# A Mamba, attention and mixture-of-experts layer in one kernel: scan and attention reordered, eight exponentials in sixteen summed on VectorE, row scatters moved, and eight buffers for the last loads

## The chip, the cores and the metric

The kernel runs as one program on 1 core of a Trainium2 chip. The metric is the device time of one execution, in microseconds (us). The program has one queue of instructions for each engine: TensorE (PE, matmuls and transposes), VectorE (DVE), ScalarE (ACT), GpSimd (POOL), and SyncE (SP), which issues most DMAs. Every queue runs in the order in which it was written and waits only on semaphores; no scheduler moves anything.

## The reference, cut to what matters

The input `x` is 32 sequences of 128 tokens of 128 numbers (4096 tokens). Three blocks follow one another, each with a residual and a layernorm.

```python
# block 1: selective state-space model, 256 channels, 16 states
xs, res = split(x @ W_in)                      # 256 + 256 columns
u = silu(conv4(xs) + conv_b)                   # causal, 4 taps, per channel
dt, Bm, Cm = split(u @ W_x)                    # 64, 16, 16
delta = softplus(dt @ W_dt + b_dt)
h[t] = exp(delta[t] * A) * h[t-1] + delta[t] * Bm[t] * u[t]     # per channel and state
y = (sum_n h * Cm + u * D) * silu(res)
x = layernorm(x + y @ W_out)
# block 2: causal attention to ctx, 16 heads of 8, rotary positions
s = rope(x @ Wq.T) . rope(ctx @ Wk.T) / sqrt(8) + masks
x = layernorm(x + softmax(s) @ (ctx @ Wv.T) @ Wo.T + bo)
# block 3: 8 experts, 2 for each token, F = 512
wte = phi_routing(x @ gate_w.T)
x = layernorm(x + sum_e wte[:, e] * ((silu(x @ w1[e].T) * (x @ w3[e].T)) @ w2[e].T))
```

## The kernel before

**Groups.** The first two blocks run over G = 8 groups of S = 4 sequences, T = 512 tokens. For group `m` the code calls `w` the group before, `e` the next and `c` the one after next, since stages of several groups overlap: while group m is scanned, the convolution of c, the step sizes of e and the routing of w are done in between.

**Scan.** The 256 channels times 16 states of 512 tokens are NU = 16 units `k`. For each, ACT makes `decays` (`decay`, L673, four exponentials of 128x256), PE makes the inputs in a pair of PSUM banks (`entries`, L1436, 16 matmuls), DVE runs the recurrence (`states`, L967), and POOL multiplies by C (`times_c`, L496). After every fourth unit PE sums over the states (`y_add`, L1458). The sets alternate: units 1, 3, 5, ... take `pair_b`, the others `pair_a`, unit 0 `y_ps`. So `entries(7)` may start when scan 5 has ended, and scan 7 may start when `entries(7)` has ended. Eight places in SBUF hold the states; scan 8 also needs that `y_add(m, 0)` has emptied the first four. PE's list puts into each step k, behind `entries(k+1)`, parts of other groups: transposes of x (`x_t`), `conv`, `res`, `b_columns`, `values`, the logits of w.

**Attention.** For each sequence t of four: `scores` puts 16 heads into four banks (pair_b and y_ps, two halves k), `maxima` (DVE, L1025) takes row maxima, `exps` (ACT, L714) takes 16 exponentials of 128x128 into `prob`, each with `accum_out`, which gives the row's sum in `den`. `head_t` (PE, L1549) transposes `prob` by four heads, `pT_out` (half on ACT, L724, half on DVE, L1040) copies them out, `heads_v` (L1570) multiplies with the values. `inverses` (DVE, L1030) and `inverses_t` prepare 1/den, `normed` applies it. PE's `scores(g, t+1, k)` overwrites the banks that the exponentials of t read, so it waits for them. The queries of sequences 2 and 3 take a path of their own: `first_norm(g, 1)` (DVE, L1009), `x1_t` (PE, L1512), `x1_in` (ACT, L702), `queries` (PE, L1518), `rope_q` (DVE, L1015), `add_q` (POOL, L501); `scores(g, 2, 0)` waits for them.

**Routing.** When the experts of group w are known, `scatter` (POOL, L528) sends each token's row to the rows of its two experts in DRAM, eight indirect DMAs for a group, issued two groups later.

**Experts.** 72 tiles of 128 rows run in a software pipeline (`up`, `down`, L1742 to L1754). At the end the two result rows of each token come back in eight groups (`results_in`, SP, L407) to four buffers `yk`; group g+4 waits until group g is summed. ACT and POOL multiply by the gates (`weighted`, L896, L585), PE sums (`sums`, L1782), DVE takes statistics (L1324, L1328), ACT the root (`ln_scale3`), and DVE writes the norm (`last_norm`, L1335), which SP stores (L411).

## Time and profile before

| what | value |
|---|---|
| device time, median of 3 runs | 1009.97 us (1008.43 to 1010.68) |
| the profiled execution: its own time | 999.74 us |
| its span | 997.8 us |
| PE busy | 872.5 us (87%) |
| PE weight loads busy | 580.5 us (58%) |
| DVE busy | 742.2 us (74%) |
| ACT busy | 719.8 us (72%) |
| POOL busy | 581.1 us (58%) |
| mean granted clock of TensorE | 0.975 |

The span goes from the first instruction to the last; the profiled execution's own time is 1.9 us longer, and the median of the timed runs lies 10.2 us above it. Busy times of engines overlap. A row of the timeline begins with the start and the duration in us; the duration of a row with x4 is that of the four together, and neighbours on one engine can overlap at their ends because they are pipelined. What stands in brackets is the engine's idle time before the row, and who ended it.

### The profile page before, as it was taken

How to read it: one execution, taken by the hardware profiler on the slowest of the kernel's cores; microseconds unless marked ns; L12 is line 12 of the kernel's file. 1: busy time of each engine (PE TensorE's matmuls, PEld its weight loads, DVE VectorE, ACT ScalarE, POOL GpSimd, SP SyncE). 2: the span in 40 equal slices, each digit the busy share in tenths (PEclk: the TensorE clock that was granted, in tenths of full speed). 3: DMA queues.
4: the chain of work that ended last, by engine and by line, in shares of the span. 5: the costliest groups of instructions: out<-in, count | busy, mean ns of one | idle time of the engine just before them, and what ended most of it. 6: DMA issues, size and time to landing. Idle time of an engine off the chain costs nothing.

```text
span 997.8 us, 29713 instructions
## 1 busy us (share of the span) xinstructions
PE 872.5 (87%) x10285; PEld 580.5 (58%) x10286; DVE 742.2 (74%) x1503; ACT 719.8 (72%) x2213; POOL 581.1 (58%) x394
## 2 busy tenths in 40 slices
PE   5578988989899798889989888988898999999996
PEld 2234554454455345445544544554588999999972
DVE  2589788878878977887897797788764666666657
ACT  3597997898799689879959985965924555555556
POOL 2588359629846973984797398397152333333331
PEclk8799999999999999999999998999999999999999
DMA  3435101500610240061033006004041111111135
GB/s 106 107 66 142 41 4 48 123 16 11 151 42 14 71 112 18 9 156 37 14 86 86 19 8 154 8 13 175 7 136 52 48 48 48 48 48 46 47 118 169
DMA packets 68476, 66.12 MB, mean 66 GB/s; under 512 B 9040, under 2 KB 62480, under 8 KB 67984
## 3 DMA queue, kind: packets, MB, share of 16 engines
q1 hardware_dynamic: 63440, 55.58, 21.5%
q0 software_dynamic: 4352, 8.99, 2.7%
q8 instruction: 69, 1.13, 0.5%
q14 instruction: 39, 0.32, 0.1%
q10 hardware_dynamic: 576, 0.10, 0.1%
HBM read 48.51 MB, written 16.13 MB: 65 GB/s over the span
## 4 chain that ended last, share of the span: by engine, by line
PE 44%; ACT 21%; DVE 18%; issue 12%; POOL 3%; DMA 2%; SPq 0%; DVEq 0%; POOLq 0%; ACTq 0%
ACT prob L714 8%; PE pair_b L1746 7%; PE pair_a L1742 7%; DVE prob L967 6%; ACT decays L673 5%; DVE hst L967 4%; PE pair_b L1538 3%; PE bank L1754 3%; PE y_ps L1754 3%; PE bank L1549 3%; DVE u L933 2%; PE pair_a L1570 2%; PE pair_a L1478 2%; PE y_ps L1538 1%; PE pair_a L1436 1%
## 5 line engine op out<-in xcount | busy, mean ns | idle before, releaser
L673 ACT ACTIVATE decays<-w,a_neg 128x256 f32<-128x256 f32 x512 | 218.7, 509 | 47.1 <-DVE prob L967 30.1
L496 POOL TENSOR_TENSOR hst<-hst,c_rep 128x1024 f32<-128x1024 f32 x64 | 151.3, 2372 | 12.6 <-DVE hst L967 12.0
L576 POOL DMA_INDIRECT y<-aoT,dest x72 | 77.3, 1074 | 135.1 <-DVE aoT L1289 131.5
L496 POOL TENSOR_TENSOR prob<-prob,c_rep 128x1024 f32<-128x1024 f32 x56 | 132.1, 2368 | 9.4 <-DVE prob L967 8.9
L528 POOL DMA_INDIRECT xg<-x_all,pos x64 | 64.9, 1014 | 88.4 <-DVE pos L1117 77.1
L714 ACT ACTIVATE prob<-pair_b,nmax 128x128 f32<-128x128 f32 x256 | 90.2, 399 | 2.1 <-DVE nmax L1025 2.1
L967 DVE TENSOR_TENSOR_SCAN prob<-decays,pair_b 128x1024 f32<-128x1024 f32 x32 | 72.8, 2276 | 24.0 <-issue 18.6
L714 ACT ACTIVATE prob<-y_ps,nmax 128x128 f32<-128x128 f32 x256 | 90.6, 413 | 0.0
L1436 PE MATMUL pair_a<-w,du_tok 64*32 64x256 f32 x1792 | 63.4, 392 | 29.8 <-DVE prob L967 15.1
L1436 PE MATMUL pair_b<-w,du_tok 64*32 64x256 f32 x2048 | 71.6, 389 | 19.5 <-DVE prob L967 12.1
L488 POOL TENSOR_TENSOR w<-diag,b_tok 128x1024 f32<-128x1024 f32 x32 | 61.9, 1959 | 37.5 <-ACT b_tok L654 23.5
L1742 PE MATMUL pair_a<-qk,u 128*128 128x128 f32 x592 | 78.2, 275 | 0.0
L1746 PE MATMUL pair_b<-qk,u 128*128 128x128 f32 x592 | 78.2, 275 | 0.0
L860 ACT ACTIVATE zabs<-pair_a 128x512 f32<-128x512 f32 x74 | 44.2, 598 | 44.7 <-PE pair_a L1742 44.7
L1549 PE MATMUL bank<-ident,prob 128*128 128x128 f32 x512 | 70.7, 279 | 5.2 <-ACT pT L724 5.2
L1549 PEld LDWEIGHTS bank<-ident,prob 128*128 128x128 f32 x512 | 55.1, 140 | 31.4 <-issue 18.4
L967 DVE TENSOR_TENSOR_SCAN hst<-decays,pair_b 128x1024 f32<-128x1024 f32 x32 | 72.6, 2269 | 0.6 <-issue 0.3
L967 DVE TENSOR_TENSOR_SCAN prob<-decays,pair_a 128x1024 f32<-128x1024 f32 x32 | 72.7, 2272 | 0.2 <-PE pair_a L1436 0.2
L1746 PEld LDWEIGHTS pair_b<-qk,u 128*128 128x128 f32 x592 | 72.0, 192 | 0.0
L1742 PEld LDWEIGHTS pair_a<-qk,u 128*128 128x128 f32 x592 | 71.9, 192 | 0.0
L1436 PEld LDWEIGHTS pair_b<-w,du_tok 64*32 64x32 f32 x2048 | 31.9, 107 | 60.1 <-DVE prob L967 27.0
L714 ACT ACTIVATION_READ_ACCUMULATOR prob<-y_ps,nmax 128x1 f32 x256 | 65.1, 254 | 0.0
(291 smaller groups left out, 2194.6 us busy)
## 6 DMA issues: line engine op xcount, KB each, us to landing
w<-d_dram SPq DMA_DIRECT2D x64, 256.0 KB, 6.5
c_rep<-c_dram SPq DMA_DIRECT2D x64, 128.0 KB, 3.8
qk<-xg SPq DMA_DIRECT2D x79, 65.0 KB
d_dram<-zpos SPq DMA_DIRECT2D x8, 512.0 KB, 3.2
xn<-in_x SPq DMA_DIRECT2D x8, 256.0 KB, 2.9
cn<-in_ctx SPq DMA_DIRECT2D x8, 256.0 KB, 3.1
mask_b<-in_mask SPq DMA_DIRECT2D x8, 256.0 KB, 3.3
w<-in_w1T SPq DMA_DIRECT2D x1, 2048.0 KB, 7.8
```

The lines of the kernel that those rows point to most:

```text
L488: last = g_.tensor_tensor(b_diag[:, t], diag64[:, :].unsqueeze(1).broadcast_to((P, NST, HK)), b_tok[:, t, :].unsqueeze(2).broadcast_to((P, ...
L496: g_.tensor_tensor(by_state(ring(k)), by_state(ring(k)), c_rep[:, :, toks[r]].rearrange("p q (i t) -> p i q t", i=2), ALU.mult).then_inc(s ...
L528: pool.indirect_dma_start(xg[:, :], bass.IndirectOffsetOnAxis(ap=pos[:, t, k:k + 1], axis=0), x2_all[:, w * S + t, :], None).then_inc(s["s ...
L576: pool.indirect_dma_start(y2[:, :], bass.IndirectOffsetOnAxis(ap=dest[:, b:b + 1], axis=0), ys[:, b % 4, :], None).then_inc(s[f"y_out{b % ...
L673: last = A(by_state(decays[:, k % 3, :])[:, :, q, :], delta_rep[:, b, toks[r]].rearrange("p (i t) -> p i t", i=2), ACT.Exp, scale=a_neg[:, ...
L714: last = A(prob[:, t % 2, c, j, :], bank[2 + c][:, j * L:(j + 1) * L], ACT.Exp, bias=nmax[:, t % 2, h:h + 1], accum_out=den[:, t % 2, h:h ...
L967: v_.tensor_tensor_scan(ring(k), decays[:, k % 3, :], pair(k)[:, :, :].rearrange("p i c -> p (i c)"), 0.0, ALU.mult, ALU.add).then_inc(s[" ...
L1436: last = MM(pair(k)[32 * j:32 * j + 32, i, :].rearrange("p (q y t) -> p q y t", q=NQ, y=2)[:, :, y, :], du_tok[half, r, y, 32 * b:32 * b + ...
L1549: last = TR(bank[6 + c % 2][:, j * L:(j + 1) * L], prob[:, t % 2, c, j, :], ident[:, :])
L1742: last = MM(bank[b][:, c * P:(c + 1) * P], w13[:, b, 0, c * P:(c + 1) * P], xsT[:, b, :], start=True, stop=True)
L1746: last = MM(bank[2 + b][:, c * P:(c + 1) * P], w13[:, b, 1, c * P:(c + 1) * P], xsT[:, b, :], start=True, stop=True)
L1754: last = MM(bank[5 + b][:, 0:P], gg[:, b, c * P:(c + 1) * P], w2[:, bass.ds(e, 1), c, :].rearrange("p a d -> p (a d)"), start=(c == 0), st ...
```

## The change

No arithmetic is dropped. Five things change.

1. **Scan.** On PE, `y_add(m, 0)` moves from step 5 to step 6, so that `entries(7)` stands ahead of it; `conv(c, 0)` goes from step 5 to 7, `conv(c, 1)` from 8 to 9, `b_columns` from 6 to 7, `res` from 11 and 13 to 12 and 13. ACT's `x_in`, `conv_out` and DVE's `taps_in` move with them.
2. **Scatters.** The four of a group that stood between POOL's first scan products move into the attention, so that all eight stand there.
3. **The way from scan to attention.** On PE, `y_add(g, 3)` goes ahead of `du_t(e, 1)` and `scores(g, 0, 1)` ahead of `residual(g, 1)`. On ACT, the silu of u and its table load go ahead of `x1_in(g, 0)`, `exps(g, 0, 0)` ahead of `duT_out(e, 1)`, `ln_scale1(g, 1)` behind `exps(g, 0, 1)`, and `x1_in(g, 1)` behind `exps(g, 1, 0)`. On DVE and PE, the first sequence's work is reordered, and the queries of sequences 2 and 3 come later in it.
4. **Sums.** For t = 1, 2, 3 the first eight exponentials leave out `accum_out`; a new DVE instruction, `sums_of_exps`, reduces their 128x1024 to 128x8, and `inverses` waits for it as well.
5. **End.** `yk` has eight buffers (four in the place of `w1`), and SP issues the eight loads ahead of all stores, without waiting.

```diff
-        yk = [x.rearrange("p k (s d) -> p (k s) d", s=S) for x in (c_rep[:, 0:2, :], u[:, 0], u[:, 1], sres[:, 0])]
+
+        yk = [x.rearrange("p k (s d) -> p (k s) d", s=S)
+              for x in (c_rep[:, 0:2, :], u[:, 0], u[:, 1], sres[:, 0], w1[:, 0:2], w1[:, 2:4], w1[:, 4:6], w1[:, 6:8])]
...
-            for b in range(4):
-                results_in(b, b)
             for g in range(G):
-                if g + 4 < G:
-                    at(sp, "acc_ps", g + 1)
-                    results_in(g + 4, g % 4)
+                results_in(g)
+            for g in range(G):
                 store(g)
             for b in range(2):
...
                 for k in range(NU - 1):
-                    if m >= 2 and k < S:
-                        scatter(m - 2, (k,))
                     times_c(m, k)
...
                 if m >= 2:
-                    scatter(m - 2, (S,))
+                    scatter(m - 2, (0,))
                 if e is not None:
                     diagonals(e, 1)
                 if m >= 2:
-                    scatter(m - 2, (S + 1,))
+                    scatter(m - 2, (1, 2, 3, 4))
                 add_q(m, 1)
                 if m >= 2:
-                    scatter(m - 2, (S + 2,))
+                    scatter(m - 2, (5,))
                 add_bo(m)
                 if m >= 2:
-                    scatter(m - 2, (S + 3,))
+                    scatter(m - 2, (6,))
                 if e is not None:
                     add_k(e)
+                if m >= 2:
+                    scatter(m - 2, (7,))
+                if e is not None:
                     masked(e)
                     mask_bias(e)
...
-            def silus(c):
+            def silus_u(c):
                 nc.scalar.preload_act_table_set("silu_and_others")
                 for h in range(2):
                     u_silu(c, h)
+
+            def silus_res(c):
                 at(act, "res_sb", 2 * (c - 2) + 2)
                 A(sres[:, c % 3], sres[:, c % 3], ACT.Silu).then_inc(s["sres_sb"], 1)
                 nc.scalar.preload_act_table_set("natural_log_exp_and_others")
...
+                    mine = {} if t and not k else {"accum_out": den[:, t % 2, h:h + 1]}
+                    last = A(prob[:, t % 2, c, j, :], bank[2 + c][:, j * L:(j + 1) * L], ACT.Exp, bias=nmax[:, t % 2, h:h + 1], **mine)
...
                 if c is not None:
                     res_out(c, 1)
+                    silus_u(c)
                 x1_in(g, 0)
                 for j in range(4):
                     own_k(g, j)
                 if e is not None:
                     duT_out(e, 0, 6)
                 if c is not None:
-                    silus(c)
+                    silus_res(c)
+                exps(g, 0, 0)
                 if e is not None:
                     duT_out(e, 1, 6)
-                exps(g, 0, 0)
+                exps(g, 0, 1)
                 ln_scale1(g, 1)
-                exps(g, 0, 1)
-                x1_in(g, 1)
...
+            def sums_of_exps(g, t):
+                at(dve, "p_sb", 16 * g + 4 * t + 2)
+                at(dve, "rden_sb", S * g + t - 1)
+                v_.tensor_reduce(out=den[:, t % 2, 0:H // 2], in_=prob[:, t % 2, 0:2].rearrange("p c j m -> p (c j) m"), axis=AX.X,
+                                 op=ALU.add).then_inc(s["den_sb"], 1)
+
             def inverses(g, t):
                 at(dve, "p_sb", 16 * g + 4 * t + 4)
+                if t:
+                    at(dve, "den_sb", (S - 1) * g + t)
...
-                first_norm(g, 1)
-                if w is not None:
-                    which(w)
                 for t in range(S):
                     if t == S - 1 and w is not None:
                         ranked(w)
                         normed(g, t - 1)
                     if t + 1 < S:
                         maxima(g, t + 1, 0)
-                    if t == 0 and e is not None:
-                        rope_k(e, 0, 0)
+                    if t == 0:
+                        first_norm(g, 1)
+                        pT_out(g, t, 1)
+                        if w is not None:
+                            which(w)
+                        if e is not None:
+                            rope_k(e, 0, 0)
                     inverses(g, t)
                     if t + 1 < S:
                         widen(g, t)
                     if t and not (t == S - 1 and w is not None):
                         normed(g, t - 1)
-                    pT_out(g, t, 1)
-                    if t == 0:
-                        rope_q(g, 1)
+                    if t:
+                        pT_out(g, t, 1)
                     if t == 1 and w is not None:
                         cast(w)
                         mark(w)
-                    if t == 0 and e is not None:
-                        rope_k(e, 1, 0)
                     if t + 1 < S:
                         maxima(g, t + 1, 1)
                     elif e is not None:
                         states(e, 0)
+                    if t == 0:
+                        rope_q(g, 1)
                     pT_out(g, t, 3)
+                    if t == 0 and e is not None:
+                        rope_k(e, 1, 0)
+                    if t + 1 < S:
+                        sums_of_exps(g, t + 1)
...
-                    if k == 5:
+                    if k == 6:
                         y_add(m, 0)
                     if k == 8:
                         values(g)
...
                         if k == 3:
                             step(e, 0, 4)
                             step(e, 1, 5)
-                        if k == 6:
+                        if k == 7:
                             b_columns(e, 7)
                         if k == 14:
                             du_t(e, 0, 6)
                     if c is not None:
-                        if k == 5:
+                        if k == 7:
                             conv(c, 0, 6)
-                        if k == 8:
+                        if k == 9:
                             conv(c, 1, 6)
...
                 scores(g, 0, 0)
+                y_add(g, 3)
                 if e is not None:
                     du_t(e, 1, 6)
-                y_add(g, 3)
+                scores(g, 0, 1)
                 residual(g, 1)
-                scores(g, 0, 1)
                 first_out(g, 1)
                 if e is not None:
                     c_t(e, 0)
                 for t in range(S):
                     if t + 1 < S:
                         scores(g, t + 1, 0)
-                    if t == 0:
-                        if e is not None:
-                            keys(e, 0, 0)
-                        x1_t(g, 1)
                     if t:
                         inverses_t(g, t - 1)
                         heads_v(g, t - 1)
...
                     head_t(g, t, 0)
                     head_t(g, t, 1)
                     if t == 0:
-                        queries(g, 1)
                         if e is not None:
-                            keys(e, 1, 0)
+                            keys(e, 0, 0)
+                        x1_t(g, 1)
                     if t + 1 < S:
                         scores(g, t + 1, 1)
                     head_t(g, t, 2)
+                    if t == 0:
+                        if e is not None:
+                            keys(e, 1, 0)
+                        queries(g, 1)
                     if t == S - 1 and e is not None:
                         entries(e, 0)
```

The next two pieces are PE in the scan, steps 4 to 7 of a middle group (L1436, now L1454: `entries`; L1593, now L1611: logits; L1445, now L1463: `y_begin`; L1458, now L1476: `y_add`, of whose eight rows two stand here). Before:

```order
L1436 MATMUL pair_a<-w,du_tok 32x4x64 x16
L1593 MATMUL bank<-gate_wT,x2T 128x8 x4
L1445 MATMUL y_ps<-u,d_diag 128x256 x2
L1458 MATMUL y_ps<-hst,sum 32x256 x2
L1458 MATMUL y_ps<-prob,sum 32x256 x2
...
L1365 MATMUL bank<-xT,w_in 128x512
L1436 MATMUL pair_b<-w,du_tok 32x4x64 x16
L1398 MATMUL bank<-ident,dtl 128x32 x4
```

Now:

```order
L1454 MATMUL pair_a<-w,du_tok 32x4x64 x16
L1611 MATMUL bank<-gate_wT,x2T 128x8 x4
L1463 MATMUL y_ps<-u,d_diag 128x256 x2
L1454 MATMUL pair_b<-w,du_tok 32x4x64 x16
L1476 MATMUL y_ps<-hst,sum 32x256 x2
L1476 MATMUL y_ps<-prob,sum 32x256 x2
...
L1454 MATMUL pair_a<-w,du_tok 32x4x64 x16
L1416 MATMUL bank<-ident,dtl 128x32 x4
L1383 MATMUL bank<-xT,w_in 128x512
L1454 MATMUL pair_b<-w,du_tok 32x4x64 x16
```

The `entries` of unit 7, into `pair_b`, stood behind `y_add` and `conv` (L1365, now L1383); now it stands ahead of both, and `b_columns` and `conv` stand behind the entries of unit 8.

The next two pieces are DVE in the attention of a middle group, first sequence (L1025, now L1030: `maxima`; L1009, now L1014: `first_norm(g, 1)`; L1015, now L1020: `rope_q(g, 1)`; L1040, now L1053: `pT_out`). Before:

```order
L1009 TENSOR_SCALAR x<-pair_a,mv,rstd 128x128 x2
L1084 MAX_INDEX i<-m_all,lg_all 128x8 x4
L1025 TENSOR_REDUCE nmax<-pair_b 128x4 x2
L983 TENSOR_TENSOR rotk<-pair_a,rope 128x512
L1030 RECIPROCAL rden<-den 128x16
L1034 TENSOR_TENSOR rden_wide<-rden,one_col 128x128
L1040 COPY pT<-bank 128x512
L1015 TENSOR_TENSOR rotq<-pair_a,rope 128x256 x2
L983 TENSOR_TENSOR rotk<-pair_a,rope 128x512
L1025 TENSOR_REDUCE nmax<-y_ps 128x4 x2
L1040 COPY hst<-bank 128x512
L1025 TENSOR_REDUCE nmax<-pair_b 128x4 x2
```

Now:

```order
L1030 TENSOR_REDUCE nmax<-pair_b 128x4 x2
L1014 TENSOR_SCALAR x<-pair_a,mv,rstd 128x128 x2
L1053 COPY pT<-bank 128x512
L1097 MAX_INDEX i<-m_all,lg_all 128x8 x4
L988 TENSOR_TENSOR rotk<-pair_a,rope 128x512
L1043 RECIPROCAL rden<-den 128x16
L1047 TENSOR_TENSOR rden_wide<-rden,one_col 128x128
L1030 TENSOR_REDUCE nmax<-y_ps 128x4 x2
L1020 TENSOR_TENSOR rotq<-pair_a,rope 128x256 x2
L1053 COPY hst<-bank 128x512
L988 TENSOR_TENSOR rotk<-pair_a,rope 128x512
L1036 TENSOR_REDUCE den<-prob 128x8
```

`first_norm` stood ahead of the maxima of the next sequence and stands behind them; `rope_q` stands behind the second maxima; and a reduction of `prob` (L1036, `sums_of_exps`) ends the piece.

The last two pieces are POOL behind the scan products (L488, now L487: `diagonals`; L528, now L527: `scatter`; L501, now L500: `add_q(g, 1)`). Before:

```order
L488 TENSOR_TENSOR w<-diag,b_tok 128x1024 x2
L528 DMA xg<-x_all,pos 33920x130
L488 TENSOR_TENSOR w<-diag,b_tok 128x1024 x2
L528 DMA xg<-x_all,pos 33920x130
L501 TENSOR_TENSOR qk<-rotq 128x256
```

Now:

```order
L487 TENSOR_TENSOR w<-diag,b_tok 128x1024 x2
L527 DMA xg<-x_all,pos 33920x130
L487 TENSOR_TENSOR w<-diag,b_tok 128x1024 x2
L527 DMA xg<-x_all,pos 33920x130 x4
L500 TENSOR_TENSOR qk<-rotq 128x256
L527 DMA xg<-x_all,pos 33920x130
```

Five scatters instead of two stand ahead of `add_q(g, 1)`.

## Rows read from the trace of the kernel before

**Rows 1.** The page's chain that ended last, shares of the span by engine.

```profile
PE 44%; ACT 21%; DVE 18%; issue 12%; POOL 3%; DMA 2%; SPq 0%; DVEq 0%; POOLq 0%; ACTq 0%
```

**Rows 2.** Busy us (count) of PE, PEld, DVE, ACT, POOL by stretch; clock, DMA, GB/s.

```profile
303.40:326.10 22.70, 21.71 (x343) 12.29 (x342) 19.32 (x25) 21.04 (x50) 18.27 (x11) 1.00 0.05 15
326.10:354.60 28.50, 21.64 (x363) 10.94 (x362) 28.05 (x26) 18.56 (x43) 25.91 (x15) 1.00 0.44 103
354.60:365.50 10.90, 9.81 (x75) 5.26 (x74) 7.64 (x27) 10.83 (x41) 9.55 (x6) 1.00 0.50 135
365.50:389.40 23.90, 22.11 (x251) 13.20 (x250) 16.47 (x39) 22.50 (x110) 8.46 (x7) 1.00 0.07 19
...
760.00:964.40 204.40, 203.33 (x1823) 203.17 (x1822) 130.62 (x443) 110.57 (x219) 77.30 (x72) 1.00 0.17 47
```

**Rows 3.** Timeline of DVE, scans: start, us, and idle time before in brackets.

```profile
326.09 2.29 DVE L967 TENSOR_TENSOR_SCAN prob<-decays,pair_b 128x1024 f32<-128x1024 f32 x1 [2.86 <-issue]
...
584.09 2.29 DVE L967 TENSOR_TENSOR_SCAN prob<-decays,pair_b 128x1024 f32<-128x1024 f32 x1 [1.80 <-issue]
...
668.21 2.29 DVE L967 TENSOR_TENSOR_SCAN prob<-decays,pair_b 128x1024 f32<-128x1024 f32 x1 [2.45 <-ACT decays L673]
```

**Rows 4.** Timeline of PE, scan of the same middle group.

```profile
321.91 0.41 PE L1458 MATMUL y_ps<-hst,sum 128*32 128x256 f32 x2
...
323.78 1.12 PE L1365 MATMUL bank<-xT,w_in 128*128 128x512 f32 x2
324.83 1.09 PE L1436 MATMUL pair_b<-w,du_tok 64*32 64x256 f32 x32
```

**Rows 5.** Timeline of POOL, same group.

```profile
319.07 2.37 POOL L496 TENSOR_TENSOR prob<-prob,c_rep 128x1024 f32<-128x1024 f32 x1
...
363.54 1.01 POOL L528 DMA_INDIRECT xg<-x_all,pos  x1 [0.17 <-issue]
367.73 0.72 POOL L501 TENSOR_TENSOR qk<-rotq 128x256 f32<-128x256 f32 x1 [3.18 <-DVE rotq L1015]
```

**Rows 6.** Timeline of ACT, same group: the way into the attention, then three of its exponentials' rows.

```profile
358.79 0.60 ACT L666 ACTIVATE du_tok<-bank 128x512 f32<-128x512 f32 x1
...
366.32 0.43 ACT L714 ACTIVATE prob<-pair_b,nmax 128x128 f32<-128x128 f32 x1
366.57 0.27 ACT L714 ACTIVATION_READ_ACCUMULATOR prob<-pair_b,nmax 128x1 f32 x1
366.66 0.44 ACT L714 ACTIVATE prob<-pair_b,nmax 128x128 f32<-128x128 f32 x1
```

**Rows 7.** Timeline of PE, attention of the same group.

```profile
362.23 0.39 PE L1531 MATMUL pair_b<-mbias,identb 128*128 128x512 bf16 x1 [0.81 <-ACT prob L714]
...
367.54 0.59 PE L1531 MATMUL y_ps<-mbias,identb 128*128 128x512 bf16 x2
...
370.57 1.13 PE L1538 MATMUL pair_b<-hst,qk 32*128 32x512 f32 x4
```

**Rows 8.** Waits of 303.4 to 389.4: total us, times, longest.

```profile
DVE nmax L1025 <- PE y_ps L1538: 2.9, 3, 1.8
...
DVE rank L1101 <- PE pair_a L1603: 2.0, 1, 2.0
...
DVE nmax L1025 <- PE pair_b L1538: 1.6, 2, 1.0
DVE hst L967 <- PE y_ps L1436: 1.6, 1, 1.6
```

**Rows 9.** Timeline of DVE at two places, a reduction and a sum of two.

```profile
963.95 0.69 DVE L1316 TENSOR_REDUCE hst<-hst 128x64 f32<-128x512 f32 x1
...
353.00 0.42 DVE L1020 TENSOR_TENSOR qk<-rotq 128x256 f32<-128x256 f32 x1
...
609.54 1.26 DVE L1020 TENSOR_TENSOR qk<-rotq 128x256 f32<-128x256 f32 x1
```

**Rows 10.** Timeline of the end: DVE's statistics.

```profile
988.79 0.89 DVE L1324 BATCH_NORM_STATS2 pT<-pair_b 128x6 f32<-128x128 f32 x4 [1.03 <-PE pair_b L1782]
```

40 lines of the change are left out of this document (20 added, 20 removed).

## The prediction

> **What bounds the kernel now.** Read the chain of waits first: it changes engine often, PE 44%, ACT 21%, DVE 18% [rows 1]. So no engine's total decides, and each stage has to be read by itself. The table of busy times by stretch comes next; I cut one middle group (303.4 to 389.4, 86.0 us) into four [rows 2]. Its second stretch, the later scan units, is DVE's: 28.05 of 28.5 us busy. Its fourth, the attention, is shared by PE (22.11 of 23.9) and ACT (22.50). In its first DVE is busy for only 19.32 of 22.7 us, and the timeline of DVE says where most of the rest is: before scan 7 it stands idle for 2.86 us [rows 3]. The granted clock is 1.00 in all four. The expert stage (204.4 us, PE busy for 203.33) is not touched by the change, so whatever is gained comes from eight groups and the last 33 us.
>
> **The scan.** DVE's idle time before scan 7 is put down to "issue", so PE's own timeline must tell the cause. There `y_add` begins at 321.91 and is followed by `conv` at 323.78 and the entries of unit 7 at 324.83; scan 7 starts at 326.09, 1.26 us after its entries [rows 3, 4]. `y_add` thus holds PE for 1.87 us and `conv` for 1.05. Scan 6 had ended at 326.09 - 2.86 = 323.23. In the new order the entries stand at 321.91 and are ready at 323.17, just in time: the wait of 2.86 us goes. What is late next is unit 8: PE does entries 7 (1.0), `y_add` (1.87) and then entries 8, ready after 1.26: 321.91 + 1.0 + 1.87 + 1.26 = 326.05, while scan 7 ends at 323.23 + 2.2 = 325.43. That is a new wait of 0.6 us before scan 8, and the net gain is 2.2 us. `conv` and `b_columns` come later, but the taps on DVE move behind scan 8 with them; I cost that at nothing, hidden by the scan in between.
>
> The same wait is 1.80 us in group 6, which has no `conv`, and 2.45 in group 7, where the profile names ACT instead [rows 3]. With 0.6 lost again that gives 1.2 and, because ACT's own exponentials are then close, 1.3.
>
> The four scatters that leave POOL's products cost 1.01 + 0.17 = 1.18 us each [rows 5], 4.7 in all. The fourth product ended at 319.07 + 2.37 = 321.44, 0.47 us before `y_add` used it, so alone this is worth nothing. It is the cover that the new order needs: without the scatters POOL is 4.7 us ahead when DVE gains 2.2.
>
> **The way into the attention.** ACT reached its first exponentials only behind `duT_out` at 358.79 [rows 6]; now that copy stands behind them and the silu of u is done before. How much earlier they start is not what counts, as long as it is more than PE waits for them. PE's row has one stall for these exponentials, 0.81 us at 362.23 [rows 7]; the rest of PE's list up to `scores(g, 2, 0)` runs nearly without gaps and keeps its length. I take 0.8 for PE, and nothing for `y_add` ahead of `du_t`, since `residual` now stands in the row that it used to precede.
>
> But `scores(g, 2, 0)` needs the queries, and these are now issued at the end of PE's list. Before, PE came to its main matmuls at 370.57 [rows 7]; 0.81 less is 369.8, and its two mask matmuls and one `head_t` (together 1.0) stand behind the queries, which therefore end at about 368.8. `rope_q` on DVE and `add_q` on POOL follow, the latter 0.72 us [rows 5], the former about the same: 370.3. So of the 0.8 us only 0.25 are left. POOL must be free for `add_q`: the second scatter begins at 363.54, and four at 1.18 end at 368.3 [rows 5], a margin of about 1.3 us.
>
> **The sums.** With `accum_out`, one exponential starts 0.34 us after the last (366.32, 366.66); its accumulator read starts 0.25 after it and costs 0.09 [rows 6]. What an exponential without the read takes, the trace does not show. Bounds: 0.34, if the read cost nothing, and below 0.25 if the read also waited for a pipeline to empty. I take 0.25, the nearest row, so a half of eight gains 0.72 us. Of the three halves in a group the first (t = 1) falls where ACT waits for PE and the queries, and gives nothing; the other two give 1.4. Below 0.25 PE is the next bound, so that end adds little.
>
> DVE pays for it. A reduction of 512 elements from SBUF took 0.69 [rows 9]; the new one has 1024, so it lies between 0.69 and 1.38, and I take 1.2, 3.6 us a group. DVE's idle time in the attention is 2.9 + 1.6 + 2.0 us for maxima and ranks, of which 1.8 lie ahead of the first sequence: 4.7 remain, and 1.6 more before the next group's scan 0 [rows 8]. So the 3.6 fit, though not wholly: each sum stands ahead of the next maxima. I subtract 0.1. Attention: 0.25 + 1.4 - 0.1, about 1.6 us a group; 1.2 in group 7, where no scan follows.
>
> DVE's sum of two SBUF tensors took 0.42 us at 353.00 and 1.26 at 609.54 [rows 9], where a POOL product was running. The Trainium skill's page SBUF — State Buffer, section Who interferes with whom, says that a DVE instruction with two SBUF inputs contends with a GpSimd one that reads SBUF, and that `tensor_reduce` never does. By that rule the new sums pay nothing to the five scatters beside them; by the opposite one each could wait for one, at 1.0 us, and the sum would be 3 us a group smaller. No row shows a reduction held up, and the estimate above stays.
>
> **The end.** Before the statistics of group 6 DVE waits 1.03 us [rows 10]; that comes from a load which SP issued late, behind a store. With all eight loads queued at once it goes, and DVE is then the bound at its own pace: 1.0 us, once.
>
> **The sum.** Groups 0 to 5: 6 x (2.2 + 1.6) = 22.8. Group 6: 1.2 + 1.6 = 2.8. Group 7: 1.3 + 1.2 = 2.5. End: 1.0. Together 29.1 us. The profiled execution took 999.74 us, which gives 970.6. The median of the runs shown lies 10.2 us above it and stays so: 1009.97 - 29.1 = 980.9, say 981.
>
> **Rivals.**
> *Attention gives nothing*: the queries' new path, one engine after the other, eats what the exponentials give. For it: that path has six hops and three of them are now later in their lists. Against: it is passed once in a group, and the two halves counted lie behind it. 6 x 2.2 + 1.2 + 1.3 + 1.0 = 16.7, giving 993.
> *The scan's stall only moves*: PE is the bound of units 4 to 9 whatever the order (21.71 of 22.7 us busy in the first stretch [rows 2]), and what scan 7 gains, scans 8 to 10 lose. Against: in the second stretch PE is busy for 21.64 of 28.5. 7 x 1.6 + 1.2 + 1.0 = 13.4, giving 997.
> *ScalarE's pace decides the attention*: PE's list gives way, and the group gains 0.8 + 3 x 0.7 + 1.0 (of the wait before scan 0), about 4 us instead of 1.6. 29.1 + 8 x 2.2 = 47, giving 963. PE's 22.11 of 23.9 us speaks against.
> *Ports*: with DVE 2.2 us ahead, its sum of two (0.42) meets POOL's last product in every group and takes 1.26 as at 609.54, 0.84 x 8 = 6.7 us more: 988. The rule of that page would have it so wherever the two overlap.
> *Slower, VectorE blocks the attention*: in order, `sums_of_exps(t+1)` must wait for ACT and stands ahead of `maxima`, for which ACT itself waits. If the sums find no idle time, 3.6 us, and the first norm and `rope_q`, each moved behind maxima, cost 1.2 more, a group changes by 3.6 + 1.2 - 2.2 = +2.6 us: 8 x 2.6 - 1.0 = +20, giving 1030. It decides from where over 2.2 us of these 4.8 come onto the path. The 4.7 us of idle time speak against it.
> *It does nothing*: the gains are smaller than what a measurement of this kernel can tell, 0.2%.
>
> **How the numbers follow.** Forecast 0.49 (973 to 988), attention nothing 0.15, stall moves 0.12, ScalarE's pace 0.09, ports 0.05, VectorE blocks 0.08, nothing 0.02. The range from 966 to 1000 holds the forecast, both half gains, the ports, and some of ScalarE's pace; it leaves out the slower case and the far end of the faster one. If an exponential without the read still takes 0.34, the sum loses 8 x 1.4 = 11 us: 992, inside. Faster: 0.49 + 0.15 + 0.12 + 0.09 + 0.05 = 0.90; same 0.02; slower 0.08.
>
> **What would show it.** In the new profile the idle time before scan 7 is gone and 0.6 us stand before scan 8. Exponentials without the accumulator start 0.25 us apart. `sums_of_exps` takes 1.2 us on DVE, 24 times. ACT waits for PE's first `head_t` of t = 1, and PE a little for `add_q`. A middle group takes 82.2 us instead of 86.0. The last eight loads leave SP in one row. The forecast is wrong if scans 8 to 10 wait for PE by more than 1 us together, if `maxima` of t = 2 or 3 starts later than its scores by more than a sum, or if `add_q` waits for POOL's scatters.

## The result, and the profile after

The median fell from 1008.49 us to 997.18 us (9 runs of each). The medians lie 11.3 us apart. The ratio is 0.9896, 95% interval 0.9874 to 0.9918: faster by 10.5 us, where the forecast had 29.1. It was right in its direction, wrong in size by a factor of nearly three, and the time lies inside the range.

Two things first, so that the numbers add up. The runs were made in several sets, and one stretch differs between them: between the positions of group 6 and those of group 7, the profile of the changed kernel and the four of experiments 1 to 4 (the first set) have 19.2 us whatever the kernel. The two profiles of the kernel before and the six others of the later sets have 12.4, and there the kernel before took 1000.6 to 1001.8 us. So times are compared only with the kernel before that ran beside them. And the changed kernel was run once more in a later set: 0.9897 (0.9881 to 0.9914), the same ratio.

Read the groups by the start of scan 0 on VectorE. The eight starts are 48.28, 127.04, 209.17, 293.70, 378.24, 464.46, 548.98 and 634.06 us; before they were 49.57, 131.80, 217.45, 303.47, 389.49, 475.94, 562.17 and 646.45. The first two groups are shorter by 3.5 us each, nearly the 3.8 of the forecast. From the third on, where routing work of an earlier group is mixed in, the gain is 1.5, 1.5, 0.2 and 1.7 us, and group 6 is 0.8 us longer. That break is the case's question.

The stretches of a middle group (293.7 to 378.2), cut at the same events as [rows 2]:

```profile
293.60:315.20 21.60, 18.78 (x309) 11.00 (x313) 21.05 (x24) 18.23 (x45) 13.67 (x6) 1.00 0.02 4
315.20:344.10 28.90, 24.60 (x398) 12.16 (x390) 28.10 (x27) 23.96 (x51) 26.42 (x15) 1.00 0.48 105
344.10:355.00 10.90, 10.43 (x80) 5.71 (x78) 7.69 (x25) 10.37 (x45) 10.18 (x7) 1.00 0.46 126
355.00:378.20 23.20, 21.19 (x248) 13.00 (x248) 19.46 (x44) 18.48 (x79) 11.73 (x11) 1.00 0.09 30
```

VectorE is now busy in 21.05 of the 21.60 us before scan 7, where it was in 19.32 of 22.7. It is full, but the stretch is only 1.1 us shorter. ACT has 18.48 of 23.2 us in the attention instead of 22.50 of 23.9. VectorE's scans around the place of [rows 3]:

```profile
315.24 2.29 DVE L972 TENSOR_TENSOR_SCAN prob<-decays,pair_b 128x1024 f32<-128x1024 f32 x1
318.12 2.29 DVE L972 TENSOR_TENSOR_SCAN hst<-decays,pair_a 128x1024 f32<-128x1024 f32 x1 [0.60 <-PE pair_a L1454]
```

The wait of 2.86 us before scan 7 is gone and 0.60 stand before scan 8, as forecast. What filled the stretch instead stands between scan 0 and scan 1 (first fence; the second has the same place in the kernel before):

```profile
293.70 2.29 DVE L972 TENSOR_TENSOR_SCAN hst<-decays,y_ps 128x1024 f32<-128x1024 f32 x1 [1.43 <-PE y_ps L1454]
295.91 0.67 DVE L1053 COPY hst<-bank 128x512 f32<-128x512 f32 x1
296.49 2.04 DVE L1121 TENSOR_TENSOR prk<-rank,oh_all 128x64 f32<-128x64 f32 x1
299.00 2.29 DVE L972 TENSOR_TENSOR_SCAN hst<-decays,pair_b 128x1024 f32<-128x1024 f32 x1
...
391.42 2.29 DVE L972 TENSOR_TENSOR_SCAN prob<-decays,pair_b 128x1024 f32<-128x1024 f32 x1 [2.04 <-issue]
```

```profile
303.47 2.29 DVE L967 TENSOR_TENSOR_SCAN hst<-decays,y_ps 128x1024 f32<-128x1024 f32 x1 [1.61 <-PE y_ps L1436]
306.25 0.21 DVE L1108 TENSOR_TENSOR prk<-rank,oh_all 128x64 f32<-128x64 f32 x1
306.93 2.29 DVE L967 TENSOR_TENSOR_SCAN hst<-decays,pair_b 128x1024 f32<-128x1024 f32 x1
```

`prk`, the product of rank and one-hot rows, has 64 elements a partition and takes 2.04 us. It took 0.21 us at 306.25 in the kernel before. POOL's timeline has the reason (the changed kernel, then the kernel before), and PE's of the next group what follows:

```profile
296.07 2.38 POOL L495 TENSOR_TENSOR hst<-hst,c_rep 128x1024 f32<-128x1024 f32 x1 [7.89 <-DVE hst L972]
```

```profile
307.22 1.06 POOL L528 DMA_INDIRECT xg<-x_all,pos  x1 [9.51 <-DVE pos L1117]
```

```profile
386.14 0.49 PE L1597 MATMUL bank<-x1b,ident 128*128 128x128 f32 x2 [2.16 <-DVE aoT L1063]
386.44 0.62 PE L1599 MATMUL bank<-woT,aoT 128*128 128x128 f32 x2
386.85 3.38 PE L1398 MATMUL y_ps<-u,w_x 128*96 128x512 f32 x4
```

```profile
387.00:391.50 4.50, 4.50 (x57) 1.72 (x62) 2.43 (x10) 1.82 (x5) 3.60 (x2) 0.68 0.00 0
```

POOL's first product runs from 296.07 to 298.45, and `prk` ends at 298.53. In the kernel before, POOL stood in front of its first scatter, which waits for the positions that VectorE makes from `prk`; so the product could not meet it. Scan 1 starts 5.30 us after scan 0 instead of 3.46. `aoT` comes behind scan 1, PE idles for 2.16 us, and in this group and in group 6 its granted clock falls to the lower level, 1.2 GHz: from 387 to 389 us it is 0.50, in the last row's stretch 0.68 on average, the four matmuls of `w_x` take 3.38 us instead of 1.88 (at 302.13 with the clock at 1.00), and scan 3 waits for 2.04 us.

The chain of waits, in the place of [rows 1], is misleading here:

```profile
POOL 35%; PE 34%; issue 24%; DVE 3%; ACT 2%; another core or an unknown queue 1%; DMA 1%; POOLq 0%; DVEq 0%; SPq 0%; ACTq 0%
```

POOL's share went from 3% to 35%, though POOL is busy for 582.2 us where it was for 581.1, and now waits for scans between its first products (2.92, 1.46 and 1.07 us). Yet an experiment that starts the first of them later makes the kernel faster.

The attention. The first row is the wait of ACT for PE, then eight exponentials without accumulator as one row; the next fence is PE's wait for `add_q`, and VectorE's sums by line:

```profile
363.07 0.60 ACT L727 ACTIVATE pT<-bank 128x512 f32<-128x512 f32 x1 [2.98 <-PE bank L1567]
363.57 2.17 ACT L718 ACTIVATE prob<-pair_b,nmax 128x128 f32<-128x128 f32 x8
365.59 0.63 ACT L727 ACTIVATE hst<-bank 128x512 f32<-128x512 f32 x1
```

```profile
360.05 1.13 PE L1556 MATMUL pair_b<-hst,qk 32*128 32x512 f32 x4 [0.78 <-POOL qk L500]
```

```profile
L1036 DVE TENSOR_REDUCE den<-prob 128x8 f32<-128x1024 f32 x24 | 29.0, 1209 | 0.0
```

Eight exponentials take 365.59 - 363.57 = 2.02 us, 0.25 each, where [rows 6] has 0.34 between starts; a sum takes 1.21, 24 times. All as forecast. The end, in the place of [rows 10], has no idle time before the statistics of group 6 any more:

```profile
987.67 0.89 DVE L1342 BATCH_NORM_STATS2 pT<-pair_b 128x6 f32<-128x128 f32 x4
```

### The profile page after: what moved, and what is told of

Its sections match the earlier page's. It is cut to its first block, busy times and chain, and to the rows that moved or that the text cites. A ratio compares the mean times of both kernels' runs of the same rounds, so it can differ in the third digit from the quotient of the medians.

```text
span 996.9 us, 29574 instructions
## 1 busy us (share of the span) xinstructions
PE 871.1 (87%) x10285; PEld 582.8 (58%) x10286; DVE 777.5 (78%) x1527; ACT 703.8 (71%) x2021; POOL 582.2 (58%) x394
## 4 chain that ended last, share of the span: by engine, by line
POOL 35%; PE 34%; issue 24%; DVE 3%; ACT 2%; another core or an unknown queue 1%; DMA 1%; POOLq 0%; DVEq 0%; SPq 0%; ACTq 0%
POOL prob L495 12%; POOL hst L495 11%; PE pair_a L1760 7%; PE pair_b L1764 7%; POOL w L487 5%; PE bank L1772 3%; PE y_ps L1772 3%; POOL xg L527 3%; PE bank L1567 3%; PE pair_b L1525 2%; POOL zabs L472 2%; PE pair_b L1556 2%; PE pair_a L1588 2%; PE y_ps L1556 2%; POOL mbias L509 1%
## 5 line engine op out<-in xcount | busy, mean ns | idle before, releaser
L1454 PE MATMUL pair_b<-w,du_tok 64*32 64x256 f32 x2048 | 71.0, 386 | 18.9 <-DVE prob L972 11.1
L527 POOL DMA_INDIRECT xg<-x_all,pos x64 | 63.8, 997 | 38.7 <-DVE pos L1130 23.7
L487 POOL TENSOR_TENSOR w<-diag,b_tok 128x1024 f32<-128x1024 f32 x32 | 61.9, 1960 | 36.9 <-ACT b_tok L656 22.9
L718 ACT ACTIVATE prob<-pair_b,nmax 128x128 f32<-128x128 f32 x256 | 74.4, 387 | 4.7 <-DVE nmax L1030 4.6
L1454 PE MATMUL pair_a<-w,du_tok 64*32 64x256 f32 x1792 | 62.0, 385 | 17.5 <-DVE hst L972 9.2
L1454 PEld LDWEIGHTS pair_b<-w,du_tok 64*32 64x32 f32 x2048 | 32.1, 107 | 61.1 <-DVE prob L972 21.8
L1476 PE MATMUL y_ps<-hst,sum 128*32 128x256 f32 x512 | 64.6, 396 | 0.9 <-POOL prob L495 0.5
```

The costliest lines, as they stand in the source:

```text
L487: last = g_.tensor_tensor(b_diag[:, t], diag64[:, :].unsqueeze(1).broadcast_to((P, NST, HK)), b_tok[:, t, :].unsqueeze(2).broadcast_to((P, ...
L527: pool.indirect_dma_start(xg[:, :], bass.IndirectOffsetOnAxis(ap=pos[:, t, k:k + 1], axis=0), x2_all[:, w * S + t, :], None).then_inc(s["s ...
L718: last = A(prob[:, t % 2, c, j, :], bank[2 + c][:, j * L:(j + 1) * L], ACT.Exp, bias=nmax[:, t % 2, h:h + 1], **mine)
L1454: last = MM(pair(k)[32 * j:32 * j + 32, i, :].rearrange("p (q y t) -> p q y t", q=NQ, y=2)[:, :, y, :], du_tok[half, r, y, 32 * b:32 * b + ...
L1476: last = MM(y_ps[32 * i:32 * i + 32, r, h * HT:(h + 1) * HT].rearrange("p (i t) -> p i t", i=2), sum32[:, :], by_state(ring(4 * x + i))[:, ...
```

## The experiments

Each kernel was timed beside the kernel before, and the ratio is to that kernel. The times in the expectations of experiments 5 to 7 were worked out from the 1008.4 us of the first set; the kernel before that ran beside them took 1000.6, so they are to be compared by the ratio.

**1. Who holds `prk`?** Theory A is the port, B another bound, C another cause on VectorE's side. First `prk` alone moves ahead of scan 0:

```
                     elif e is not None:
+                        if w is not None:
+                            spots(w)
                         states(e, 0)
...
```

> The changed kernel with one DVE instruction moved: the product of rank and one-hot rows (two SBUF inputs, 128x64) stands before scan 0 of the next group, where POOL is idle, and no longer behind it, where POOL's first product runs. Theory A (the two share a port: 2.04 us instead of 0.21, six times, and in groups 4 and 6 the late aoT lets the granted clock fall, 1.7 us each): the product takes 0.21 us again, scan 1 starts about 3.3 us after scan 0 instead of 5.30, and the time is 983 to 986 us, 11 to 14 below the changed kernel's 997.2. Rival B (the missing gain lies elsewhere: PE or POOL sets the pace of the scan, the sums of exponentials cost what they save): the product gets shorter but a later scan waits for as long, and the time stays within 995 to 998.

Measured: 993.13 us, ratio 0.9849 (0.9824 to 0.9874). Better than the change, but less than theory A's number, and more than B's. VectorE's timeline, then POOL's, in the group of scan 0 at 376.73:

```profile
378.94 0.67 DVE L1053 COPY hst<-bank 128x512 f32<-128x512 f32 x1
379.52 0.21 DVE L1125 TENSOR_REDUCE posf<-prk 128x8 f32<-128x64 f32 x1
379.76 1.74 DVE L1130 CAST pos<-posf 128x8 int32<-128x8 f32 x1
381.42 2.27 DVE L972 TENSOR_TENSOR_SCAN hst<-decays,pair_b 128x1024 f32<-128x1024 f32 x1
```

```profile
379.10 2.38 POOL L495 TENSOR_TENSOR hst<-hst,c_rep 128x1024 f32<-128x1024 f32 x1 [7.88 <-DVE hst L972]
```

`prk` took 0.21 us in its new place. But the next instruction in the row is now beside POOL's product (379.10 to 381.48): the reduction `posf` took 0.21 and was not held; the cast to `pos`, eight elements with one SBUF input, took 1.74, to 381.50. So theory A is right about what `prk` waited for, and the move only handed the wait to the next instruction that the product can hold.

**2. Take the overlap away on POOL's side.** Nothing moves; POOL only starts later.

```
                 for k in range(NU - 1):
+                    if m >= 2 and k == 0:
+                        at(pool, "pos_sb", m - 1)
                     times_c(m, k)
```

> The changed kernel with one wait added and nothing moved: POOL starts its first product of a group only when DVE has written the positions (as the scatter ahead of it made it do in the kernel before). Theory A (shared port): the added wait makes the kernel faster, DVE's product takes 0.21 us again, and the time is 983 to 987 us. Rival C (the 2.04 us have another cause on DVE's side, such as the producer of its inputs): the product stays at 2.04 us, POOL starts its products about 3 us later than in the changed kernel, and the time is 997 to 1002. Rival B (pace set elsewhere): 996 to 999.

Measured: 987.09 us, 0.9791 (0.9767 to 0.9815). An added wait gained another 10.1 us. VectorE, then POOL:

```profile
374.46 2.29 DVE L974 TENSOR_TENSOR_SCAN hst<-decays,y_ps 128x1024 f32<-128x1024 f32 x1 [1.43 <-PE y_ps L1456]
377.25 0.21 DVE L1123 TENSOR_TENSOR prk<-rank,oh_all 128x64 f32<-128x64 f32 x1
...
377.93 2.29 DVE L974 TENSOR_TENSOR_SCAN hst<-decays,pair_b 128x1024 f32<-128x1024 f32 x1
```

```profile
378.00 4.68 POOL L495 TENSOR_TENSOR hst<-hst,c_rep 128x1024 f32<-128x1024 f32 x2 [9.05 <-DVE pos L1132]
```

`prk` takes 0.21, scan 1 follows scan 0 by 3.47, and each middle group takes 82.70 us; the forecast had 82.2. C falls. So does B: POOL idled 9.05 us before its products and the scans kept their pace.

It was run again in a later set, beside the changed kernel.

> The changed kernel with POOL's wait for the positions, once more, beside the changed kernel and the one with the old way on the same chip. Theory A: 10 us below the changed kernel, as before (0.979 against 0.990); the kernel with early positions was 0.58 us a group better by its profile, so its further gain of 0.9% was partly the chip's, and the ratio here is 0.975 to 0.979.

> The changed kernel once more. If the stretch between the positions of group 6 and group 7 depends on the chip and not on the kernel, it takes 12.4 or 19.2 us here as in the others of this call, and the ratio to the kernel before stays at 0.990, within 0.002.

Measured: 975.33 us, 0.9745 (0.9732 to 0.9759), and 991.12, 0.9897. The two ratios of the waiting kernel, 0.9791 and 0.9745, differ by more than their intervals. Of the 11.1 us between its two profiles 6.9 are the stretch named above, 0.7 stand in group 7 and 3.4 in the experts and the end, where the two profiles of the kernel before also differ by 2.0; what moves the experts is open. So by the medians the port costs the change 10 or 16 us. By the profiles, from the first scan 0 to the positions of group 6, which leaves the experts out, it costs 13.0 in the first set and 12.7 in the later one. These 12.7 part so: groups 2 to 5 lose 1.8 us each, two of them 1.7 more by the clock (0.66 from 303 to 307, 0.70 from 474 to 478), groups 6 and 7 lose 0.3 and 1.7.

**3. The scatters alone.** The kernel before with only POOL's part of the change, whose value the forecast put at nothing.

```
                 for k in range(NU - 1):
-                    if m >= 2 and k < S:
-                        scatter(m - 2, (k,))
                     times_c(m, k)
...
```

> The kernel before with one part of the change: the scatters leave POOL's products of the scan and stand in the attention. Theory A: POOL's first product now starts right after scan 0, DVE's product of rank and one-hot rows takes 2.0 us, and aoT comes 1.8 us late. PE, which was busy in 21.7 of 22.7 us there, comes late to y_add by as much: 6 x 1.8 = 11 us slower than the kernel before, about 1019. Rival D (the 2.86 us that DVE idled before scan 7 swallow it): the product takes 2.0 us, the wait before scan 7 shrinks to about 1, and the time stays within 1007 to 1010. Rival C: product at 0.21 us and no change.

Measured: 1025.61 us, 1.0160 (1.0136 to 1.0184), 17 us slower, where theory A had 11. Rival D had the 2.86 us of idle time swallow the delay. VectorE, then PE:

```profile
396.83 2.04 DVE L1109 TENSOR_TENSOR prk<-rank,oh_all 128x64 f32<-128x64 f32 x1
...
418.50 2.29 DVE L968 TENSOR_TENSOR_SCAN prob<-decays,pair_b 128x1024 f32<-128x1024 f32 x1 [2.86 <-issue]
```

```profile
401.96 0.46 PE L1580 MATMUL bank<-x1b,ident 128*128 128x128 f32 x2 [2.17 <-DVE aoT L1051]
```

`prk` takes 2.04, and the 2.86 us before scan 7 are all still there: that wait is for PE, and PE itself came late by its wait for `aoT` (2.17 us). Groups 2 to 5 take 88.7, 88.6, 88.1 and 90.1 us, 1.6 to 3.8 more than before; scan 1 comes 1.8 later. In groups 2 and 3 a fall of PE's clock behind the last scan goes with the rest (0.58 from 254 to 258 us, 0.50 from 344 to 346), which the kernel before has not in those two.

**4. The scan's new order alone**, with the scatters left between POOL's products.

```
-                    if k == 5:
+                    if k == 6:
                         y_add(m, 0)
...
-                        if k == 5:
+                        if k == 7:
                             conv(c, 0, 6)
...
```

> The kernel before with one part of the change: y_add, conv, res and what belongs to them stand one or two scan units later on PE, ACT and DVE; the scatters stay between POOL's products. My forecast's term: 2.2 us in each of seven groups, 16 us less if nothing else binds, 992. Rival E (the scatters are the cover that the new order needs: POOL's products ran without a gap from 319 to 350 us and its last waited only 0.44 us for a scan): DVE's idle time before scan 7 goes, but later scans wait for POOL's products, and a group gains 0.5 to 1 us, 1001 to 1005.

Measured: 1006.49 us, 0.9967 (0.9949 to 0.9986). Rival E had the number nearly right and the place wrong: the stretch from scan 0 to the last scan is 44.0 us instead of 46.6, so the gain is all there, and no scan waits for POOL. It is lost behind the last scan (VectorE, then POOL):

```profile
431.66 1.74 DVE L1020 TENSOR_TENSOR qk<-rotq 128x256 f32<-128x256 f32 x1
...
435.56 0.69 DVE L1025 TENSOR_REDUCE nmax<-pair_b 128x4 f32<-128x512 f32 x1 [1.03 <-PE pair_b L1538]
```

```profile
430.76 2.34 POOL L496 TENSOR_TENSOR prob<-prob,c_rep 128x1024 f32<-128x1024 f32 x1
```

`add_q` on VectorE, 0.42 us at [rows 9], meets POOL's last product and takes 1.74. PE's scores wait 1.74 us for it instead of 0.49, and behind that wait PE's granted clock is 0.50 for 6 us (PE here, then in the kernel before, then the stretch here):

```profile
433.45 2.08 PE L1538 MATMUL pair_b<-hst,qk 32*128 32x512 f32 x4 [1.74 <-DVE qk L1020]
```

```profile
353.55 1.13 PE L1538 MATMUL pair_b<-hst,qk 32*128 32x512 f32 x4 [0.49 <-DVE qk L1020]
```

```profile
433.45:439.45 6.00, 6.00 (x36) 2.61 (x40) 2.37 (x3) 5.96 (x15) 4.68 (x3) 0.50 0.89 194
```

From the last scan to the next scan 0 the groups take 41.9 to 43.4 us instead of 39.4. PE's `y_add(g, 3)`, which reads POOL's last product, is not what waits: the product ends at 433.10, and `y_add` begins at 436.50. In the kernel before that product had ended at 350.23 + 2.37 = 352.60, 0.4 us before `add_q`; POOL, with four scatters still among its products, cannot follow the faster scans. The forecast called the scatters' move a cover that the new order needs: it is, and in this run `add_q`, held by POOL's late product, is where it is needed.

**5. Both parts of the scan, and POOL's wait.** The edits of 2, 3 and 4 on the kernel before; attention and end stay.

```
+                    if m >= 2 and k == 0:
+                        at(pool, "pos_sb", m - 1)
                     times_c(m, k)
...
-                    if k == 5:
+                    if k == 6:
                         y_add(m, 0)
```

> The kernel before (median 1008.4) with the scan's part of the change and nothing else: y_add, conv and res later, the scatters in the attention, and POOL's wait for the positions, so that nothing meets on the port. The attention and the end stay as before. My forecast's term for the scan is 2.2 us in each of six groups, 1.2 and 1.3 in the last two, 15.7 together: 992.7. Rival H (later scans lose part of it): 996 or more. In the profile the idle time before scan 7 is gone, 0.6 us stand before scan 8, and a middle group takes 83.8 us.

Measured: 982.40 us, 0.9817 (0.9804 to 0.9830), 18.2 us faster by the medians. A middle group takes 83.50 us. The scan's part was worth more than the forecast's 15.7, not less: 2.5 us a group instead of 2.2.

**6. The sums of the exponentials taken out** of the kernel of experiment 2.

```
-                    mine = {} if t and not k else {"accum_out": den[:, t % 2, h:h + 1]}
+                    mine = {"accum_out": den[:, t % 2, h:h + 1]}
...
-                    if t + 1 < S:
-                        sums_of_exps(g, t + 1)
...
```

> The changed kernel with POOL's added wait (987.1 us), and the sums of exponentials given back to ScalarE (accum_out for all heads, no sums on VectorE). My forecast's term: two of three halves of eight save 0.72 us each, less 0.1, so about 1.3 us a group and 8 x 1.3 = 10.7 us more than with the sums: 997 to 999. Rival F (PE's list bounds the attention, the sums give nothing): 986 to 988. Rival G (the sums stand in the way on VectorE and cost time): under 985.

Measured: 984.89 us, 0.9845 (0.9832 to 0.9859). Its middle groups take 83.42 us, with the sums they take 82.70: 0.72 us a group, half of the 1.4 of the forecast. By the ratios (0.9791 and 0.9745 with the sums) they are worth 0.5 to 1.0%. And 83.42 is also, within 0.1, what experiment 5 has with the old way into the attention. So the new way is worth nothing: in both, PE's scores of t = 2 begin 18.9 us before scan 0. Why the sums give half shows in ACT's copies for t = 2 and t = 3, here in the kernel of experiment 7, which has the sums:

```profile
358.05 0.60 ACT L727 ACTIVATE pT<-bank 128x512 f32<-128x512 f32 x1 [2.98 <-PE bank L1571]
...
364.35 0.60 ACT L727 ACTIVATE pT<-bank 128x512 f32<-128x512 f32 x1 [0.36 <-PE bank L1571]
```

With the sums one sequence takes 364.35 - 358.05 = 6.30 us, without them 6.79 (361.67 to 368.46 in this experiment). ACT saved 0.72 and then waits 0.36 for PE, whose `head_t` comes no earlier; without the sums there was no wait, and neighbours overlapped by 0.13. t = 3 gives 0.24 more.

**7. A better version.** The whole routing step, product, sum and cast, goes ahead of scan 0, where POOL is idle; no wait on POOL.

```
                     elif e is not None:
+                        if w is not None:
+                            spots(w)
+                            spot_sum(w)
+                            spots_out(w)
                         states(e, 0)
...
```

> The changed kernel with the product, its sum and the cast to positions (0.64 us of VectorE) all ahead of the next group's scan 0, where POOL is idle, and no wait added on POOL. None of them can meet a POOL product there. Theory A: VectorE had 1.4 us of idle time there, so they cost nothing, and between scan 0 and scan 1 stands only the copy of 0.67 us: scan 1 starts 2.9 us after scan 0 and a group is 0.5 us shorter than with POOL's wait (987.1): 982 to 985. Rival I (after the earlier product the next scans wait for PE, which is the bound there): 986 to 989. Rival J (the cast waits for the last scatter and delays scan 0): 989 or more.

Measured: 970.10 us, 0.9700 (0.9687 to 0.9713), 30.5 us below the kernel before beside it, and faster than both kernels. The ratio is also better than any of the expected times; by it the kernel would take 978 us in the first set, and theory A had 982 to 985.

```profile
372.20 0.17 DVE L1130 CAST pos<-posf 128x8 int32<-128x8 f32 x1
373.21 2.29 DVE L972 TENSOR_TENSOR_SCAN hst<-decays,y_ps 128x1024 f32<-128x1024 f32 x1 [0.84 <-PE y_ps L1458]
376.06 2.29 DVE L972 TENSOR_TENSOR_SCAN hst<-decays,pair_b 128x1024 f32<-128x1024 f32 x1
```

The cast takes 0.17, VectorE still idles 0.84 us before scan 0, and scan 1 follows by 2.85. Middle groups take 82.12 us, 0.58 less than in experiment 2; over the groups that is some 3 us of the 4.5 by which the ratios differ.

**8. The same, with the old way into the attention** on PE, ACT and VectorE.

```
...
                 scores(g, 0, 0)
-                y_add(g, 3)
                 if e is not None:
                     du_t(e, 1, 6)
+                y_add(g, 3)
+                residual(g, 1)
                 scores(g, 0, 1)
-                residual(g, 1)
...
```

> As the kernel with the positions computed early (ratio 0.970), except that the way from the scan into the attention is the old one on all three engines (duT_out, silus, residual, first norm, queries, keys in their old places); the sums of exponentials, the scatters in the attention, the later y_add and the eight loads stay. Theory M: the reordered way gives nothing, since scores of t=2 come at the same distance before scan 0 in both (18.92 us), and costs 2.2 us in the last group, so this kernel is 2 us faster than that one: ratio 0.968. Rival N (my forecast's 0.25 us a group, and more once the sums are there): up to 4 us slower, ratio 0.972 to 0.974.

Measured: 970.92 us, 0.9697 (0.9682 to 0.9711): no difference. The new way gives nothing in the middle (82.18 against 82.12 us), and theory M's 2.2 us in the last group was wrong too: from its scan 0 to the positions of group 6 it takes 79.6 us, 80.0 with the new way, and 78.1 in the kernel of experiment 5. What goes with that difference is PE's clock on the way into the last attention, here in this kernel and then in that of experiment 5, each from 36.0 us after scan 0:

```profile
655.88:659.88 4.00, 3.29 (x42) 1.36 (x46) 4.00 (x5) 1.03 (x3) 3.20 (x3) 0.50 0.29 53
659.88:663.88 4.00, 4.00 (x34) 1.86 (x26) 1.74 (x2) 1.05 (x2) 3.54 (x3) 0.67 0.81 328
```

```profile
664.54:668.54 4.00, 2.73 (x61) 1.52 (x65) 4.00 (x5) 1.59 (x5) 3.33 (x2) 1.00 0.26 49
668.54:672.54 4.00, 2.82 (x22) 1.25 (x14) 3.97 (x6) 2.56 (x4) 3.44 (x3) 1.00 0.86 356
```

At 0.50 and 0.67 granted, PE is busy for 7.29 of 8 us; in the same stretch at 1.00 for 5.55. With the new way and no sums (experiment 6) the clock is 0.79 over these 8 us. So the fall is there with the sums and the old way, and for less long with the new way and no sums; what brings it is not shown.

**9. The kernel before, once more**, profiled only.

> The kernel before, profiled once more: its profiled execution took 999.74 us, its timed ones 1006 to 1012. If the usual execution is some 8 us longer, this profile shows where. Theory K: after the last group, between the positions of group 6 and of group 7, where every other profile shows 19.2 us and that one 12.4. Theory L: in the groups, by stretches with TensorE at its lower clock.

Measured: 1001.35 us, and 12.37 us in that stretch. So neither theory as written: its groups are those of the first profile, and its stretch too. The kernel before has no profile with 19.2 us; its longer timed runs are those of the first set, in which all five profiles have them. There ACT began its copy of `x2T` only after 6.73 to 6.76 us of waiting (first row, the changed kernel), in the later sets after 2.15 (second row, the same kernel):

```profile
729.04 0.60 ACT L740 ACTIVATE x2T<-bank 128x512 f32<-128x512 f32 x1 [6.75 <-remote]
```

```profile
723.24 0.60 ACT L740 ACTIVATE x2T<-bank 128x512 f32<-128x512 f32 x1 [2.15 <-PE bank L1605]
```

What held it by name ("remote") the profile does not show. The record gives the same chip number for experiments 1 to 4 and for one of the later sets, so the chip alone does not decide it. The cause stays open; within a set it is the same for every profile, and no ratio rests on it.

## Why the prediction was wrong, by its steps

By profiles in which that stretch takes 12.4 us (starts of scan 0, then the positions of group 6), against the forecast's sum; "before" is its second profile, "changed kernel" that of the later set:

| term | forecast | measured | from |
|---|---|---|---|
| scan, groups 0 to 6 | -14.4 | -17.4 | experiment 5 against before |
| way in, groups 0 to 6 | -1.8 | -0.2 | 6 against 5 |
| sums, groups 0 to 6 | -9.4 | -4.3 | 2 (again) against 6 |
| port, groups 0 to 6 | 0 | +10.9 | changed kernel against 2 (again) |
| group 7, to the positions | -2.5 | +1.4 | changed kernel against before |
| end | -1.0 | -1.1 | from the statistics of group 2 to the last norm, changed kernel against before |
| sum | -29.1 | -10.7 | |

The two spans differ by 10.6 us (999.4 and 988.8). Outside the table the changed kernel is 0.8 shorter ahead of the first scan 0 and 0.7 longer in the experts, where the two profiles of the kernel before differ by 1.9.

**The step that failed** is the sentence on POOL: "so alone this is worth nothing. It is the cover that the new order needs". It priced the scatters by their length and asked who waits for the products. It did not ask what the first scatter had kept apart, so the sum has the port at nothing; the runs show 10.9 us in groups 0 to 6 and 1.7 in group 7. Its wait for the positions was also a guard that kept POOL's first product off VectorE's `prk`. By itself the move costs 17 us (experiment 3); in the changed kernel it takes back 10 to 16 by the medians, some 13 by the profiles.

The rival "Ports" had the mechanism and the wrong place: it looked at VectorE's sum of two behind the last scan, which took 0.42 to 0.43 in seven of its eight places of the changed kernel and 1.47 only in group 6. It names no other instruction with two SBUF inputs: `prk` has 64 elements and took 0.21 us. The rule quoted from the Trainium skill's page SBUF — State Buffer, section Who interferes with whom, would have found it: a VectorE instruction with two SBUF inputs contends with a GpSimd one that reads SBUF, the shared ports are an exclusive lock, and a reduction never contends. The trace agrees on all three: `prk` is held to 0.08 us behind the product's end, `posf` and the sums (1.21 us, 24 times) are not held. The same section of the Trainium skill says that a copy or cast can contend as well, when its operands allow a mode that uses both ports, which the forecast left out; experiment 1's cast of 1.74 us fits that, though the profile does not show the mode.

**The sums** were mis-sized by half. Both inputs were right (0.25 us a start, 1.2 us a sum), but the forecast took the two halves of t = 2 and t = 3 as fully on ACT's path, with PE the bound only "below 0.25". ACT waits for PE at once: a sequence takes 6.30 us, where ACT alone would have come to 6.79 - 0.72 = 6.07.

**The way in** was forecast at 0.25 us and gave 0.02: the hop chain of queries, `rope_q`, `add_q` and scores kept its time, with 0.78 us of PE's wait for `add_q` in it. The wait of ACT for PE (2.98 us) was forecast and is there.

**Group 7** was to gain 2.5 and lost 1.4. Its steps are -2.7 (experiment 5 against before), +2.2 (6 against 5), +0.2 (2 again against 6) and +1.7 for the port. With the 2.2 goes the granted clock on the way into the last attention; it is 0.57 in 674.3 to 678.3 us of the changed kernel's second profile. The forecast counted no clock at all, as all four stretches of [rows 2] had 1.00.

**Right** were the idle time before scan 7 and the 0.6 us before scan 8, with 2.5 us a group instead of 2.2; the end; the exponentials' pace; and POOL's scatters, for which `add_q` did not wait. Of the three signs named as showing the forecast wrong, none appeared. They all watched the waits that the change adds, and none the pairs of instructions that it brings side by side. The sign that did fail is the middle group: 84.5 us in groups 2, 3 and 5 of the first profile and 86.2 in group 4, with the clock's fall, where 82.2 were forecast.

**Luck.** That the time lies in the range is in part luck. The rival "The scan's stall only moves" had 997, the measured number, but its mechanism is absent: scans 8 to 10 of the middle group wait 0.60 us together. And the scan's gain, 3.0 us above the forecast, hides part of what the sums missed.

## What to carry to other kernels

Before a wait is moved, list what both engines do while it lasts: a wait that costs nothing can be what keeps two instructions apart. With VectorE and GpSimd at work together, search VectorE's row for every instruction with two SBUF inputs and every copy or cast, the shortest first, and ask which of GpSimd's long ones will run beside it in the new order: each can grow to the length of that one. Put them where GpSimd is idle; if that can't be, a wait on GpSimd may be cheaper than none.

## What the runs showed of the hardware

- VectorE instructions of 0.2 us took 1.74 to 2.05 us beside a GpSimd product of 2.37: a product of two SBUF inputs, and a cast of eight elements. A reduction between them took 0.21.
- It happens elsewhere too. In groups 2 to 6 of the changed kernel the cast to `idxf` (L1102, eight elements) takes 0.72 us instead of 0.16 and ends at 364.96, 0.04 behind a GpSimd sum (363.65 to 364.92). In the kernel of experiment 7 it takes 0.72 as well, and `add_q` of group 6 takes 2.06. What these cost is not shown.
- PE's wait for `aoT`, 2.16 to 2.17 us, stands in groups 2 to 7 of the changed kernel. Behind it the granted clock was 0.74 and 0.71 in two groups (388.0 to 391.5, 558.5 to 562.0) and 1.00 in two others (219 to 224, 474 to 479): the same wait does not always cost the same.
- One stretch after the last group takes 12.4 us in some sets of runs and 19.2 in another, the same for all kernels profiled in a set; the cause is open.
